# An early-fusion layer (patch tokens, fast-weight attention, routed experts): where and when the down weights are split into high and low parts

## What is computed

```
h = concat([patch_tokens(x), txt], axis=1)
h = h + attn(layernorm(h))        # fast weights: fw = 0.95 * fw + 0.1 * gate * k0 v0^T, of batch 0 only
h = h + ffn(layernorm(h))         # 8 experts of width 384, top 2 of each token

# ffn
g = einsum('td,efd->tef', xf, gate_w);  u = einsum('td,efd->tef', xf, up_w)
hid = silu(g) * u * (probs * top2_mask)
y = einsum('tef,edf->td', hid, down_w)
```

## Time and profile before

| | us |
|---|---|
| median of 3 runs (545.66 to 548.88) | 547.34 |
| the profiled execution | 546.67 |
| its span | 545.0 |
| TensorE busy | 482.8 (89%) |
| VectorE busy | 375.4 (69%) |
| ScalarE busy | 304.6 (56%) |
| GpSimd busy | 194.4 (36%) |

### The profile page before, as it was taken

How to read it: one execution, slowest core, us unless ns; L and a number is a source line. 1 busy time by engine, 2 the same in 40 slices (tenths; PEclk the granted TensorE clock), 3 DMA queues, 4 the chain that set the end, 5 groups by cost and what they waited for, 6 DMA issues and landing times.

```text
span 545.0 us, 12569 instructions
## 1 busy us (share of the span) xinstructions
PE 482.8 (89%) x3157; PEld 459.7 (84%) x3158; DVE 375.4 (69%) x1293; ACT 304.6 (56%) x773; POOL 194.4 (36%) x280
## 2 busy tenths in 40 slices
PE   1999998999788987799999999999999999999900
PEld 1999997877576876789999999999999999999800
DVE  4969996359979988857665665665665655665597
ACT  5484967548588885435444444444444444444473
POOL 1000000005667777764333333333333333333330
PEclk9999999999899998899999999999999999999965
DMA  8988123811333342262222222222222222225897
GB/s 304 413 351 356 24 93 94 313 45 44 106 109 118 95 128 78 91 173 72 79 75 68 78 75 68 76 77 68 76 76 68 76 77 68 71 81 154 258 354 232
DMA packets 61695, 71.67 MB, mean 132 GB/s; under 512 B 19057, under 2 KB 55730, under 8 KB 60642
## 3 DMA queue, kind: packets, MB, share of 16 engines
q1 hardware_dynamic: 49920, 51.43, 30.5%
q0 software_dynamic: 8592, 17.75, 9.0%
q10 hardware_dynamic: 3154, 2.15, 1.2%
HBM read 49.43 MB, written 21.86 MB: 131 GB/s over the span
## 4 chain that ended last, share of the span: by engine, by line
PE 73%; DVE 14%; DMA 5%; ACT 4%; issue 2%; ACTq 1%; SPq 0%; DVEq 0%; POOL 0%; POOLq 0%
PE bank L839 8%; PE pair L839 6%; PE bank L1089 5%; PE bank L1085 5%; PE bank L1088 5%; PE bank L1087 5%; PE bank L1086 5%; PE bank L1096 5%; PE pair L1105 4%; PE bank L1105 4%; PE pair L984 4%; PE pair L1074 3%; PE pair L988 3%; ACT yall L743 2%; DMA ydram<-ysb,dnow 2%; PE bank L918 2%
## 5 line engine op out<-in xcount | busy, mean ns | idle before, releaser
L776 POOL DMA_INDIRECT disp<-xf,posu x82 | 83.6, 1019 | 151.9 <-ACT xf L654 124.9
L1576 DVE TENSOR_TENSOR hh<-sg,bank 128x384 f32<-128x384 f32 x89 | 49.3, 554 | 99.5 <-ACT sg L724 99.5
L813 POOL DMA_INDIRECT ydram<-ysb,dnow x89 | 88.2, 991 | 70.6 <-DMA ydram<-ysb,dnow 36.5
L724 ACT ACTIVATE sg<-bank 128x384 f32<-128x384 f32 x89 | 43.7, 491 | 116.9 <-PE bank L1089 116.9
L1085 PE MATMUL bank<-wa,xh 128*128 x178 | 67.5, 379 | 0.0
L1089 PE MATMUL bank<-wa,xl 128*128 x178 | 60.4, 340 | 0.0
L1088 PE MATMUL bank<-wa,xh 128*128 x178 | 59.9, 337 | 0.0
L1086 PE MATMUL bank<-wa,xh 128*128 x178 | 59.7, 336 | 0.0
L1087 PE MATMUL bank<-wa,xl 128*128 x178 | 59.7, 336 | 0.0
L810 POOL COPY dnow<-dest 128x1 uint32 (+1 forms) x89 | 16.4, 185 | 105.9 <-DVE ysb L1586 96.5
L839 PE MATMUL bank<-wcT,imgT 128*128 128x193 f32 x240 | 42.5, 340 | 11.1 <-DMA imgT<-in_pixels 11.1
(11 more groups left out here) (263 smaller groups left out, 1170.9 us busy)
## 6 DMA issues: line engine op xcount, KB each, us to landing
xs<-disp SPq DMA_DIRECT2D x89, 96.0 KB, 1.9
band<-in_bands SPq DMA_DIRECT2D x4, 1536.0 KB, 12.1
yall<-ydram SPq DMA_DIRECT2D x7, 768.0 KB, 7.1
imgT<-in_pixels SPq DMA_DIRECT2D x4, 768.0 KB, 12.8
imgT<-in_pixels SPq DMA_DIRECT2D x2, 1536.0 KB, 16.2
hres<-in_text SPq DMA_DIRECT2D x1, 3072.0 KB, 26.1
wa<-in_gate_up_w SPq DMA_DIRECT2D x8, 384.0 KB, 8.5
ring<-in_gate_up_w SPq DMA_DIRECT2D x32, 96.0 KB
```

Source lines behind the costliest of these rows:

```text
L776: pool.indirect_dma_start(disp, bass.IndirectOffsetOnAxis(ap=posu[c % XBUF][:, 2 * j + k:2 * j + k + 1], axis=0), xfd[c % XBUF][:, j, :], None
L813: pool.indirect_dma_start(ydram, bass.IndirectOffsetOnAxis(ap=dnow[b][:], axis=0), ysb[r][:], None).then_inc(s_ys[b], 16)
```

## The change

The load of the raw down weights is issued by SP right behind the fourth image band, with a wait for the row sums that free its room. GpSimd, behind its constants, waits for that load and then casts and subtracts in four parts of 128x1152. The units of ScalarE and VectorE are now only the 24 of the gate and up weights, over the same nineteen turns. The ring loads' waits are renumbered, and TensorE waits for the down parts with their own semaphore.

```diff
--- before.py
+++ after.py
@@ -80,8 +80,8 @@
 POOL_SETUP = 5
 XC = D + NE
 AC = XC + NE
-DOWN_UNITS = 4
-UNITS = DOWN_UNITS + 3 * NE
+DOWN_PARTS = 4
+UNITS = 3 * NE
 RING = 3
 PATCH_BANK = (0, 1, 5, 6)
 PROJ_BANK = (4, 7, 2, 3)
@@ -314,6 +314,7 @@
         s_e, s_pf, s_pos, s_upd = (sem(n) for n in ("onehots", "prefix_mm", "positions", "residual_ready"))
         s_scat = [[sem(f"scattered{p}_{j}") for j in range(4)] for p in range(XBUF)]
         s_hi, s_lo, s_cnt = sem("expert_high"), sem("expert_low"), sem("counts_ready")
+        s_dhi, s_dlo = sem("down_high"), sem("down_low")
         s_cread, s_tab, s_zf = sem("counts_mm"), sem("table"), sem("tail_zeroed")
         s_upper, s_zpool = sem("late_uppers_scattered"), sem("rows_behind_experts_zeroed")
         s_xs = [sem(f"xs_in{i}") for i in range(DEPTH)]
@@ -376,8 +377,7 @@
             return 32 * (c // XBUF)
 
         def unit(n):
-            k = n - DOWN_UNITS
-            return None if k < 0 else (k // 3, k % 3)
+            return n // 3, n % 3
 
         def turn_units(t):
 
@@ -435,15 +435,16 @@
                     pixels_in(5, slice(6, 8), slice(0, 4))
                     sp.dma_start(aw[:], attn_w).then_inc(s_attw, 16)
 
+            sp.wait_ge(s_red, 2)
+            sp.dma_start(wd4[:, :, 1, :].bitcast(F32), down_w).then_inc(s_rawd, 16)
             sp.wait_ge(s_sq, 30)
             sp.wait_ge(s_pat, PTILES)
-            sp.dma_start(wd4[:, :, 1, :].bitcast(F32), down_w).then_inc(s_rawd, 16)
             for e in range(NE):
                 sp.dma_start(wa5[:, e, 1].bitcast(F32), gu_w[0:P, e]).then_inc(s_rawm[e], 16)
             sp.wait_ge(s_kv, 4 * NH)
             for r in range(2 * NE):
                 if r >= RING:
-                    sp.wait_ge(s_lo, DOWN_UNITS + 3 * ((r - RING) // 2) + (r - RING) % 2 + 2)
+                    sp.wait_ge(s_lo, 3 * ((r - RING) // 2) + (r - RING) % 2 + 2)
                 for half in range(2):
                     sp.dma_start(ring[r % RING][64 * half:64 * half + 64, :], gu_w[P:D, r // 2, r % 2]).then_inc(s_rawr[r % RING], 16)
 
@@ -664,20 +665,14 @@
                     norm_tile(c, j)
 
             def high(n):
-                if unit(n) is None:
-                    if n == 0:
-                        act.wait_ge(s_rawd, 16)
-                    g = slice(6 * n, 6 * n + 6)
-                    ins = nc.scalar.copy(wd4[:, g, 0, :], wd4[:, g, 1, :].bitcast(F32))
+                e, k = unit(n)
+                if k == 0:
+                    act.wait_ge(s_rawm[e], 16)
+                    ins = nc.scalar.activation(wa5[:, e, 0], wa5[:, e, 1].bitcast(F32), ACT.Copy, scale=nwab[:, 0:1])
                 else:
-                    e, k = unit(n)
-                    if k == 0:
-                        act.wait_ge(s_rawm[e], 16)
-                        ins = nc.scalar.activation(wa5[:, e, 0], wa5[:, e, 1].bitcast(F32), ACT.Copy, scale=nwab[:, 0:1])
-                    else:
-                        r = 2 * e + k - 1
-                        act.wait_ge(s_rawr[r % RING], 32 * (r // RING + 1))
-                        ins = nc.scalar.activation(wa5[:, e, 2, k - 1], ring[r % RING][:], ACT.Copy, scale=nwab[:, 1:2])
+                    r = 2 * e + k - 1
+                    act.wait_ge(s_rawr[r % RING], 32 * (r // RING + 1))
+                    ins = nc.scalar.activation(wa5[:, e, 2, k - 1], ring[r % RING][:], ACT.Copy, scale=nwab[:, 1:2])
                 ins.then_inc(s_hi, 1)
 
             act.wait_ge(s_kgr, 1)
@@ -760,6 +755,14 @@
 
             pool.affine_select(out=ltri[:], in_=ltri[:], compare_op=ALU.is_gt, fill=0.0, base=0,
                                pattern=[[1, P]], channel_multiplier=-1).then_inc(s_cons, 1)
+
+            pool.wait_ge(s_rawd, 16)
+            for n in range(DOWN_PARTS):
+                w = NE * FC // DOWN_PARTS
+                high, raw = (wd4[:, w * n:w * n + w, k, :] for k in range(2))
+                pool.tensor_copy(high, raw.bitcast(F32)).then_inc(s_dhi, 1)
+                pool.wait_ge(s_dhi, n + 1)
+                pool.tensor_tensor(raw, raw.bitcast(F32), high.bitcast(F32), ALU.subtract).then_inc(s_dlo, 1)
 
 
             def behind_tensor(i, j):
@@ -1051,6 +1054,7 @@
 
             keep_busy(bank[0], WARM[1])
             pe.wait_ge(s_lo, UNITS)
+            pe.wait_ge(s_dlo, DOWN_PARTS)
             pe.wait_ge(s_tab, 1)
 
             gate_reg = [pe.alloc_register(f"gate_expert{b}") for b in range(2)]
@@ -1434,19 +1438,15 @@
 
             def low(n):
                 v.wait_ge(s_hi, n + 1)
-                if unit(n) is None:
-                    raw = wd4[:, 6 * n:6 * n + 6, 1, :]
-                    ins = v.tensor_tensor(raw, raw.bitcast(F32), wd4[:, 6 * n:6 * n + 6, 0, :].bitcast(F32), ALU.subtract)
+                e, k = unit(n)
+                if k == 0:
+                    raw = wa5[:, e, 1]
+                    ins = v.scalar_tensor_tensor(out=raw, in0=raw.bitcast(F32), scalar=nwab[:, 0:1],
+                                                 in1=wa5[:, e, 0].bitcast(F32), op0=ALU.mult, op1=ALU.subtract)
                 else:
-                    e, k = unit(n)
-                    if k == 0:
-                        raw = wa5[:, e, 1]
-                        ins = v.scalar_tensor_tensor(out=raw, in0=raw.bitcast(F32), scalar=nwab[:, 0:1],
-                                                     in1=wa5[:, e, 0].bitcast(F32), op0=ALU.mult, op1=ALU.subtract)
-                    else:
-                        both = wa5[64:P, e, 2, k - 1, :]
-                        ins = v.scalar_tensor_tensor(out=both, in0=ring[(2 * e + k - 1) % RING][64:P, :], scalar=nwab[64:P, 1:2],
-                                                     in1=both.bitcast(F32), op0=ALU.mult, op1=ALU.subtract)
+                    both = wa5[64:P, e, 2, k - 1, :]
+                    ins = v.scalar_tensor_tensor(out=both, in0=ring[(2 * e + k - 1) % RING][64:P, :], scalar=nwab[64:P, 1:2],
+                                                 in1=both.bitcast(F32), op0=ALU.mult, op1=ALU.subtract)
                 ins.then_inc(s_lo, 1)
 
             mask(0)
```

## The result

| | us | runs |
|---|---|---|
| before | 547.22 (545.66 to 548.88) | 4 |
| after | 553.74 (552.83 to 555.65) | 4 |

The ratio is 1.0123 (95% interval 1.0083 to 1.0164): slower by 1.2%. The profiled execution of the changed kernel took 553.37 us with a span of 551.6, 6.6 us more than before.

What follows compares the result with a forecast made beforehand. Bound by a chain of waits: TensorE's patch matmuls to 89.6 us, then VectorE, then the chunk loop from 112. 546.67 + 7.3 + 1.0 - 4.1 = 550.9 profiled, 551.5 median; own range 549 to 557, 8-in-10 range 542.5 to 557.

Steps and rivals of the forecast that it cites:

- the lock: From 79.65 us: VectorE instructions with two SBUF inputs wait while GpSimd reads SBUF; patch 8 read 7.3 us late.
- rival 1: GpSimd's reads don't hold VectorE up, or only by fractions; whole gain stays, 543.2 us (544.9 if clock falls); chance 0.32.
- rival 2: GpSimd's reads hold VectorE up, but cheaply: delay 2.3 to 4.5 us, time 545.5 to 548; chance 0.13.
- The layout: GpSimd and VectorE instructions laid side by side from 79.8 us: GpSimd ends at 94.60, patch 8 is read at 97.0.
- The clock: TensorE, idle while patch 8 is late, may return at the low level: 0 to 1.7 us, taken as 1.0.
- The removal: Chunk loop: four casts off ScalarE and four subtractions off VectorE, gaining 2.4 to 4.1 us, taken as 4.1.
- late splits on the path: Chunk 1 to 2: VectorE's splits delay residuals to 139.08 us, though TensorE's sums are ready at 136.96; gain 2.4.
- the five splits: VectorE's splits in a row in chunk 1, before chunk 2's residuals, 4.75 us; four of 2.75 us would replace them.
- Rival 3: End of loop: the gap in GpSimd's scatter stream stays, rows stay at 229.7, only 1.2 us won: 546.1; chance 0.08.

## Why the prediction was right

It forecast 551.5 us and slower, for the lock; 553.74 was measured. The full range of 542.5 to 557 was so wide that rival 1 would have been inside it too; what bears the forecast out is its own range (549 to 557) and the waits in the trace. Point by point:

- **The load** was to be there at about 79.8 and cost 0. GpSimd began at 80.25, and the load by itself changed nothing (ratio 0.9993).
- **GpSimd's instructions** were taken as 1.1 and 2.0 us, 14.0 in all; they are 1.14 and 2.62, and 15.2. The cast was right. The subtraction was put too low; the estimate of 2.5 us from the Trainium skill (GPSIMD Engine Reference, Performance versus the Vector engine) was nearer. That the time by this estimate, 553.5, is close to the 553.74 measured is luck: its delay of 9.3 us is 1.3 too long.
- **The lock** was the step on which the sign hung, inferred from the other direction. The trace shows it: waits that end with GpSimd's instruction. The rival without it named 543.2, and that is what was measured where GpSimd only writes (543.33) or works 15 us later (543.05). The Trainium skill (SBUF — State Buffer, Who interferes with whom) has the rule, for two SBUF inputs on VectorE's side, and the trace agrees, with 1.91 us for an instruction of 0.16. The delay was 7.99 us, not 7.3, which also rules out rival 2 (2.3 to 4.5). That the two are so close is in part luck. The layout let GpSimd wait for VectorE as well, which put its end 0.8 us too late; it had GpSimd's work 1.2 us too short and its start 0.45 too early.
- **The argument for rival 1** from the down subtractions, equally long beside scatters, said nothing of instructions that read 1152 elements, as the prediction itself remarked.
- **The clock** behind the delay was to cost 1.0; it cost 1.21 to mask 0. The 1.6 us between mask 4 and the first expert slot were not in the sum, 0.67 of them in the keep-warm matmuls at the low level. Those, with 0.7 more for the lock and 0.2 more for the clock, less 0.1 more of gain, make 2.4 of the 2.5 us by which the profiled execution (553.37) is over the sum (550.9).
- **The removal** was to gain 2.4 us by mask 3 and 1.7 by mask 4, to 10.5 and 10.0 us a turn. It gained 2.48 and 1.76, to 10.44 and 9.90, and all of it reached the end in the versions that keep it. The reason for the 2.4 (late splits on the path) is shown by these versions. The reason for the 1.7 is only half shown: the clock fell in chunk 3 in both traces with the five splits (kernel before, 11.66 us; load alone, 12.60), but also in three of the ten traces with four (there the turn took 11.5 to 11.6 us). The shorter turn makes the fall rarer here, and does not exclude it.
- **Rival 3** did not come up: first rows were loaded 5.74 us later than before, and the slot began 6.52 later, so the keep-warm matmuls stayed the later road.

## What to carry to other kernels

Before moving elementwise work to an idle GpSimd, list what VectorE does in that stretch: each of its instructions with two SBUF inputs can wait for the end of the GpSimd instruction that is reading, so the price is up to the whole of GpSimd's time less VectorE's slack (here 7.99 us, of 15.2 less 3.07), and not zero. Scalings with one SBUF input waited here too, even for memsets. Look for a stretch where VectorE reads PSUM or waits, or cut the GpSimd instructions short, since a wait lasts for one of them; but that took GpSimd 23.8 us in place of 15.2, and the time came out at 546.29 us against 543.05 for the later stretch. And a gap on the busy engines themselves, found in the timeline, may hold the work just as well: here 10 us of casts and subtractions fitted into gaps of 2 to 4 us each.

## What the hardware showed that was not expected

- In the changed kernel the wait is one-sided: GpSimd's pitch was 3.80 us, and 3.79 in the version where it works from 95 us, while VectorE's small instructions ended 0.00 to 0.04 us behind GpSimd's. In other versions GpSimd waited too, for about 0.13 us: five of the 24 casts of 128x192 took 0.47 to 0.48 us instead of 0.34, all of them beside VectorE's groups of four normalisations, and of the four casts of 128x1152 alone the longest took 1.27 instead of 1.14.
- A VectorE instruction with a single SBUF input waited too: a scaling of 128x7 took 2.59 us, to the end of GpSimd's subtraction. Scalings of 128x1 in the stretch (0.15), a reduction (0.16) and a reciprocal of 128x7 (0.20) did not.
- GpSimd's memsets of 128x1152 all took 1.06 us (17.78 for 16 in a row), and VectorE's instructions with two SBUF inputs beside them did not wait. Its scalings with one SBUF input did, of 128x4 for up to 0.9 us.
- TensorE's clock fell in places that no edit explains: the 80 keep-warm matmuls, the same in every kernel, took between 10.57 and 11.85 us, by how long the clock was at 0.50 in them.
